# Projections and attention scores as fp16 half products, heads stacked by DMA, denominators from a ones column, no dummy matmuls

## What is computed

```python
x = x + conv(group_norm(x))          # two-way state scans over rows and columns, gated
t = tokens(x)                        # 16 x 1024 x 192
t = t + attn(layer_norm(t))
t = t + ffn(layer_norm(t))  # 4 experts 192 -> 768 -> 192, the best 2 per token, weighted
# attn: six heads of 32; token 0 sees all tokens, every other one sees token 0 and a window of 33
Q, K, V = x @ Wq + bq, x @ Wk + bk, x @ Wv + bv
s_rest  = einsum('bhld,bhlwd->bhlw', Q[:, :, 1:], Kw) / sqrt(32), masked
out     = concat(softmax(s_cls) @ V, softmax(s_rest) @ Vw) @ Wo + bo
```

## Time and profile before

| | us |
|---|---|
| median of three runs (lowest, highest) | 3214.75 (3212.38, 3215.9) |
| the profiled execution | 3210.95 |
| its span, first to last instruction | 3209.2 |
| TensorE busy in the span | 2742.2 (85%) |
| VectorE busy | 1883.9 (59%) |
| ScalarE busy | 1060.5 (33%) |
| GpSimd busy | 906.1 (28%) |

### The profile page before, as it was taken

The page is one execution under the profiler, slowest core; times in us unless marked ns, Lnnn a source line. Parts: engine busy times, 40 slices in busy tenths (PEclk is TensorE's granted clock), DMA queues, the critical chain, the costliest instruction groups (busy, mean ns, idle before and its releaser), DMA issues. The chain is left out here.

```text
span 3209.2 us, 50697 instructions
## 1 busy us (share of the span) xinstructions
PE 2742.2 (85%) x18097; PEld 2020.8 (63%) x18097; DVE 1883.9 (59%) x5344; ACT 1060.5 (33%) x3333; POOL 906.1 (28%) x672
## 2 busy tenths in 40 slices
PE   0478888998898999988998999998898989999597
PEld 0356575766667676666666676766667666766364
DVE  4454555666666566666656566566656566565464
ACT  0032423234242424334242424334242424334122
POOL 0001203050422415050422415050422415050544
PEclk9787978899998989999999989899998999899799
DMA  3430103132242415132242415133232415133564
GB/s 40 95 103 15 56 15 97 35 83 57 74 92 59 104 56 111 36 79 61 73 89 63 104 55 110 32 83 63 72 89 61 107 52 109 36 83 70 136 158 99
DMA packets 272634, 241.80 MB, mean 75 GB/s; under 512 B 209020, under 2 KB 250494, under 8 KB 261760
## 3 DMA queue, kind: packets, MB, share of 16 engines
q1 hardware_dynamic: 211648, 147.17, 17.9%
q0 software_dynamic: 50880, 52.59, 9.7%
q10 hardware_dynamic: 9856, 38.80, 3.8%
HBM read 133.29 MB, written 73.59 MB: 64 GB/s over the span
## 5 line engine op out<-in xcount | busy, mean ns | idle before, releaser
L1504 PE MATMUL PSUM<-XT,WB 128*128 128x512 f16 x2010 | 528.2, 396 | 24.5 <-DMA META<-slots 24.5
L795 ACT ACTIVATE HF<-PSUM,WB 128x512 f32<-128x512 f32 x402 | 275.8, 686 | 799.5 <-PE PSUM L1504 796.5
L1522 PE MATMUL PSUM<-WB,HHI 128*128 128x192 f16 x1608 | 404.2, 251 | 75.6 <-DVE HLO L1043 74.3
L818 ACT ACTIVATE PSPT<-PSUM,NMX 94x126 f32<-94x126 f32 x1056 | 366.9, 358 | 307.7 <-PE PSUM L1563 250.2
L1040 DVE TENSOR_SCALAR HHI<-HF 128x512 f16<-128x512 f32 x402 | 180.7, 450 | 407.3 <-ACT HF L795 404.2
L693 POOL DMA_INDIRECT out_dram<-Y,META x228 | 359.4, 1576 | 200.9 <-DVE Y L1068 117.6
L1524 PE MATMUL PSUM<-WB,HLO 128*128 128x192 f16 x1608 | 404.3, 251 | 0.0
L1523 PE MATMUL PSUM<-WB,HHI 128*128 128x192 f16 x1608 | 404.3, 251 | 0.0
L1504 PEld LDWEIGHTS PSUM<-XT,WB 128*128 128x128 f16 x2010 | 199.3, 103 | 197.6 <-issue 37.6
L1551 PE MATMUL PSUM<-KBD,QT 128*94 128x378 f32 x704 | 291.0, 495 | 18.8 <-ACT PSPT L818 17.2
L1043 DVE SCALAR_TENSOR_TENSOR HLO<-HF,HHI 128x512 f16<-128x512 f32 x402 | 282.6, 703 | 13.8
(11 more groups left out here) (269 smaller groups left out, 4978.5 us busy)
## 6 DMA issues: line engine op xcount, KB each, us to landing
WB<-weights SPq DMA_DIRECT2D x67, 1600.0 KB, 7.0
XR<-in_x ACTq DMA_DIRECT2D x16, 768.0 KB, 5.8
out_dram<-X ACTq DMA_DIRECT2D x32, 384.0 KB, 2.4
weights<-WB ACTq DMA_DIRECT2D x4, 1600.0 KB, 6.4
GUP<-TGU SPq DMA_DIRECT2D x256, 8.0 KB, 1.8
slots<-XROW,IDX POOLq DMA_INDIRECT x256, 2.4
out_dram<-Y,META POOLq DMA_INDIRECT x228, 3.6
HF<-in_w ACTq DMA_DIRECT2D x6, 384.0 KB, 4.6
```

The lines of the kernel that those rows point to most:

```text
L795: act.activation(HF[:, k % 2, :], PSUM[:, 4 + k % 2, :], ACT.Gelu, scale=1 / (X_UP * W_UP), bias=bias).then_inc(f["gelu_done"], 1)
L818: e = act.activation(PS[0:QS, n % 2, h, :], PSUM[0:QS, n % 2, h * KS:(h + 1) * KS], ACT.Exp, bias=NMX[:, b, n % 2, h:h + 1], accum_out=DEN ...
L1504: mm = pe.matmul(dst, WB[:, ws, w:w + 128], XT[:, xs, chunk, :], start=(n == 0), stop=(n == 4))
L1522: pe.matmul(dst, HHI[:, k % 2, tok], w2h, start=False, stop=False, skip_group_check=True)
```

## The change

- **Halves.** VectorE writes XN as fp16 rows of an upper half and the rest (XNR). TensorE turns these (24 fp16 transposes in place of 16 in f32), and XW holds three chunks of 128 rows. The weights are split in the same way once, at the start (WQKV).
- **Projections.** Each product is five fp16 matmuls (`X_CHUNK`) in place of two in f32.
- **Evacuation.** ScalarE evacuates all twelve Q and K pieces, each twice: as f32 (QKF) and as the upper fp16 half. VectorE subtracts them to get the lower half (`split_qk`) and evacuates all six V pieces, 33 columns for each head, of which the last stays at one.
- **Moves.** KBD is gone. `qk_moves` on SyncE copies the halves of each head into QST (upper, upper, lower) and KST (upper, lower, upper), stacked to 96 rows: 36 DMAs an image, in four groups of nine after the splits 3, 6, 9 and 12. The attention waits for all of them.
- **Scores.** The mask comes first, then one fp16 matmul for each head, 126 columns.
- **Denominators.** The exponentials no longer accumulate. The ones column of VW gives the sums with the values; VectorE copies token 0's row of them and takes the reciprocal from PSUM, behind the values.
- **Dummies.** The `keep_busy` of the attention is gone. That of image 0's conv stays.
- `STEPS` and the `empty` steps are shifted a little, and some buffers share space (XNR and the halves of K lie in X2 and XN).

```diff
-        STEPS = [(1, 1) if n < 16 else (2, 1) if n < 20 else (2, 2) for n in range(NSEL * HK)] + [(1, 1)]
+        STEPS = [(1, 1) if n < 16 else (2, 1) if n < 18 else (2, 2) for n in range(NSEL * HK)] + [(1, 1)]
...
+        X_CHUNK = (0, 0, 1, 2, 1)
...
+        def evacuate_qk(act, n):
+
+            oh, parts = piece_parts(n)
+            bias, scale = (BQS, HD ** -0.5 * UNSCALE) if n < 6 else (BK, UNSCALE)
+            for ps, plain, hi, lo in parts:
+                act.activation(plain, ps, ACT.Identity, bias=bias[:, oh:oh + 1], scale=scale)
+                last = act.activation(hi, ps, ACT.Identity, bias=bias[:, oh:oh + 1], scale=scale)
+            last.then_inc(s["piece_act"], 1)
+
+        def split_qk(dve, n):
+
+            for ps, plain, hi, lo in piece_parts(n)[1]:
+                last = dve.tensor_tensor(lo, plain, hi, ALU.subtract)
+            last.then_inc(s["qk_split"], 1)
...
+            def qk_moves(i):
+                for to, halves, rows in ((QST, [QHL[:, :, 0], QHL[:, :, 1]], (0, 0, 1)), (KST, KHL, (0, 1, 0))):
+                    for oh in range(2):
+                        sp.wait_ge(s["qk_split"], at("qk_split", i, 3 * oh + (3 if to is QST else 9)))
+                        for h in range(HH):
+                            for g, v in enumerate(rows):
+                                sp.dma_start(to[g * HD:(g + 1) * HD, oh * HH + h, :, :],
+                                             halves[oh][h * HD:(h + 1) * HD, v, :, :]).then_inc(s["qk_moved"], 16)
...
                 state_moves(i + 1)
                 expert(i, 3)
+                qk_moves(i + 1)
...
+                for k in range(2):
+                    tiles = slice(4 * k, 4 * k + 4)
+                    dve.wait_ge(s["xn1_ready"], at("xn1_ready", i, k + 1))
+                    link(dve.tensor_scalar(XNR[:, tiles, 0:C], XN[:, tiles, 0:C], X_UP, None, ALU.mult))
+                    dve.scalar_tensor_tensor(XNR[:, tiles, C:2 * C], XN[:, tiles, 0:C], X_UP, XNR[:, tiles, 0:C],
+                                             ALU.mult, ALU.subtract).then_inc(s["xnr_ready"], 1)
...
                 def normalize(b):
-                    dve.wait_ge(s["exp_done"], at("exp_done", i, 2 * b + 2))
-                    link(dve.reciprocal(RDEN[:, b, :, :], DEN[:, b, :, :]))
                     dve.wait_ge(s["pv_done"], at("pv_done", i, b + 1))
...
+                    dve.tensor_copy(DEN[:, b, :, :].rearrange("p a h -> p (a h)"), o[0:1, :, HD])
+                    link(dve.reciprocal(RDEN[:, b, :, :].rearrange("p a h -> p (a h)"), o[:, :, HD]))
...
-                    for j in range(2):
-                        mm = pe.matmul(PSUM[0:HC, n % 4, 0:width], W[:, j, oh * HC:(oh + 1) * HC],
-                                       XW[:, j, b0:b1, keys], start=(j == 0), stop=(j == 1))
+                    for m, c in enumerate(X_CHUNK):
+                        mm = pe.matmul(PSUM[0:HC, n % 4, 0:width], WQKV[:, kind, m, oh * HC:(oh + 1) * HC],
+                                       XW[:, c, b0:b1, keys], start=(m == 0), stop=(m == 4))
...
+                pe.wait_ge(s["qk_moved"], at("qk_moved", i, PER["qk_moved"]))
...
-                    pe.matmul(PSUM[0:QS, n % 2, 0:HH * KS], QT[:, oh, b, :],
-                              KBD[:, oh, b, :, :].rearrange("p h k -> p (h k)"), start=True, stop=False)
...
-                    pe.matmul(PSUM[0:QS, n % 2, 0:HH * KS], EYEB[:], MASKB[:, v, :], start=False, stop=True
-                              ).then_inc(s["score_done"], 1)
+                    pe.matmul(PSUM[0:QS, n % 2, 0:HH * KS], EYEB[:], MASKB[:, v, :], start=True, stop=False,
+                              skip_group_check=True)
+                    for h in range(HH):
+                        mm = pe.matmul(PSUM[0:QS, n % 2, h * KS:(h + 1) * KS], QST[:, oh * HH + h, b, :],
+                                       KST[:, oh * HH + h, b, :], start=False, stop=True, skip_group_check=True)
+                    mm.then_inc(s["score_done"], 1)
...
-                        keep_busy(8 if b == 1 else 2)
```

More of the change, by code:

```diff
@@ L30 @@
 QS = QB + 1
+VC = HD + 1
 E, HID = 4, 768
@@ L461, in hybrid_kernel, with windows @@
         STEPS_AHEAD = 1
-        STEPS = [(1, 1) if n < 16 else (2, 1) if n < 20 else (2, 2) for n in range(NSEL * HK)] + [(1, 1)]
-        def windows(copy, j, part, give):
+        STEPS = [(1, 1) if n < 16 else (2, 1) if n < 18 else (2, 2) for n in range(NSEL * HK)] + [(1, 1)]
+        def windows(copy, c, part):
             if part == 0:
[L469 to L475, removed]
+                return copy(XW[:, c, 1:NB - 1, 0:KW],
+                            window_view(PSUMH, c * T + QB - PAD + 1, [128, [QB, NB - 2], [1, KW]]))
+            copy(XW[:, c, 0, PAD - 1:KW], window_view(PSUMH, c * T, [128, [1, KW - PAD + 1]]))
+            copy(XW[:, c, NB - 1, 0:T - LAST_KEY], window_view(PSUMH, c * T + LAST_KEY, [128, [1, T - LAST_KEY]]))
+            return copy(XW[:, c, :, KW], window_view(PSUMH, c * T, [128, [0, NB]]))
@@ new lines, in piece_parts @@
+        def piece_parts(n):
+            src, oh, (b0, b1) = bank(n % 4), n // 3 % 2, SPANS[n % 3]
+            k, w = b1 - b0, QB if n < 6 else KS
+            hi, lo = ((QHL[:, v, oh, b0:b1, 1:QS] if n < 6 else KHL[oh][:, v, b0:b1, :]) for v in range(2))
+            plain = QKF[:, n % 2, 0:k * w].rearrange("p (b q) -> p b q", b=k)
+            parts = [(src[0:HC, 0:k * w].rearrange("p (b q) -> p b q", b=k), plain, hi, lo)]
+            if n < 6 and n % 3 == 2:
+                parts.append((src[0:HC, 400:401].broadcast_to((HC, NB)), QKF[:, n % 2, k * w:k * w + NB],
+                              QHL[:, 0, oh, :, 0], QHL[:, 1, oh, :, 0]))
+            return oh, parts
@@ L1202, in gates @@
                 dve.wait_ge(s["route_exp"], at("route_exp", i, 0))
+                if not (isinstance(i, int) and i == B):
+                    dve.wait_ge(s["mixed"], at("mixed", i, 1))
                 link(dve.tensor_reduce(sm1, se, AX.X, ALU.add))
@@ L1448, in conv @@
                         yield
-                yield from empty(4)
+                yield from empty(6)
                 pe.wait_ge(s["mixed"], at("mixed", i, NT))
@@ L1462, in conv @@
                     yield
-                yield from empty(3)
+                yield from empty(4)
                 pe.wait_ge(s["win_act"], at("win_act", i, 1))
@@ L1767, with thirds @@
     mask[0, 0, :, KW] = 0.0
+    def thirds(w):
+        w = w.reshape(3, C // 3, -1)
+        return np.stack([np.concatenate([w[p], w[q]], 0) for p, q in ((0, 1), (2, 0), (1, 2))], 1)
     w1, w2 = a["L1_ffn_w1"], a["L1_ffn_w2"]
@@ L1785 @@
         scan_v=sv, scan_u=su, scan_a=sa,
-        wq=halves(a["L1_attn_Wq"]), wk=halves(a["L1_attn_Wk"]), wv=halves(a["L1_attn_Wv"]), wo=np.concatenate([halves(a["L1_attn_Wo"]), wo_rows]),
+        wqkv=np.stack([thirds(a["L1_attn_W" + n]) for n in "qkv"], 1), wo=np.concatenate([halves(a["L1_attn_Wo"]), wo_rows]),
         bq=vec(a["L1_attn_bq"]), bk=vec(a["L1_attn_bk"]), bv=vec(a["L1_attn_bv"]),
```

196 lines of the change are left out of this document (105 added, 91 removed).

## The result

The changed kernel takes 3424.78 us (median of four runs, 3417.75 to 3426.27) against 3213.57 us (3209.22 to 3215.9): 1.0655 times, 95% interval 1.0635 to 1.0674. It is slower by 211 us. The profiled execution took 3426.27 us, its span is 3423.4 us, and TensorE's mean granted clock fell from 0.920 to 0.767.

A forecast was written before the change was run, and what follows sets the result against it. TensorE was taken to bound projections and attention. Fourteen images at -9.8 + 6.8 + 9.5 + 2.5 = +9.0 us (+126), plus +29 for images 0 and 1, gave 3370 us; forecast's own range 3310 to 3430, overall 3110 to 3440.

The forecast's parts named there:

- Projections: Projections stretch: eight matmul units become five, so it shortens from 33.4 to 23.5 us, -9.8 us an image.
- The moves: Ahead of the attention: 36 SyncE moves at 0.64 us each make TensorE wait 6.8 us an image.
- The clock: Attention: TensorE at half clock from the start, turns of 4.5 us, 56.2 us in all, +9.5 us.
- The rest: Stretches behind the attention and ahead of the projections: cold start and longer low clock, 1.7 to 3.5 us, value 2.5.
- the splits: Two VectorE splits into halves ahead of the transposes, some 1.5 us each: costed at 0, up to +3 in the range.
- The swinging between the levels: Attention: the clock swings between its levels instead of staying low, giving only part of the +9.5 us.
- The branch not taken: Attention at full clock: VectorE bounds turns of 3.3 to 3.5 us, 45.2 us in all, -1.5 us.
- The sum: Steady image: -9.8 + 6.8 + 9.5 + 2.5 = +9.0 us; images 0 and 1 +14.3 each; 3370 us in all.
- A: Rival: neither wait for moves nor fall of the clock, -10.8 us an image, 3045 us; chance 0.12.
- D: Rival: moves hidden at 0.43 us each, clock still falls, +2.7 us an image, 3260 us; chance 0.16.
- B: Rival: moves late but the attention's clock holds, -4.5 us an image, 3153 us; chance 0.10.
- E: Rival: moves at 0.96 us, or clock down through the 24.9 us behind the attention, 3510 to 3540 us; chance 0.08.

The follow-up runs named there:

- run 1: Changed kernel with the moves and the wait for them kept for image 0 alone, no dummies in the ring: 3290.22 us.
- Run 6: Changed kernel with the same 36 moves, each carrying 6 of the 11 windows (55% of the bytes): 3423.84 us.
- run 8: Changed kernel with dummies back (eight in the first turn, two in others) and eight of 36 moves done as VectorE copies: 3255.67 us.
- run 9: As run 8, with ScalarE's load of the next pixels held until the moves have landed: 3294.23 us.
- run 2: Changed kernel with the dummies back in the ring (eight in the first turn, two in the others), moves and wait unchanged: 3307.43 us.
- run 3: Changed kernel with moves for image 0 alone and the dummies back in the ring: 3170.59 us.
- run 5: Kernel before with the fp16 projections alone (halves, fp16 transposes, five matmuls), no moves, f32 scores and dummies kept: 3146.26 us, 0.9814 times the kernel before.
- run 10: As run 5, with the transposes of the halves one step later in the order: 3115.57 us, one run.
- run 12: The kernel of run 10 again, timed in five rounds: 3126.87 us, 0.9732 times the kernel before.
- run 4: Kernel before without the 28 dummies of each attention, f32 scores kept: 3239.22 us.

## Why the prediction was right, point by point

- **Projections: right.** Predicted 23.5 us for the 18 pieces with the FFN beside them, -9.8 (its terms, 15.1 and 8.2, add up to 23.3); measured 23.6 in every steady image. ScalarE's double evacuation fits, as computed: it is busy 16.69 us and the pieces wait for nothing.
- **The moves: right, a little small.** First move 5.9 us after the start of the projections, 0.64 each, landing 1.4 later, a wait of 6.8; measured 5.5, 0.675, 1.9 and 8.1. For the landing would have given 1.7 (2.3 less the 0.60 in the queue). Of the 8.1 us, 1.5 are no price of the moves, since run 1 has them too; the prediction has no such term. Run 6 shows that the price is per DMA, and the nearest row gave it well, in a range of waits from 0.5 to 18. The Trainium skill (DMA: Bandwidth & Descriptors, Issuing engines are not separate DMA queues) calls the time to initiate a DMA usually small beside the DMA. Here it is the bound: 0.675 us for each of 36 moves in a row, where the last lands 1.9 us after its issue. Its other sentence, that DMAs of all issuing engines interleave on the same 16 DMA engines, agrees with runs 8 and 9: beside ScalarE's load the last move lands after 4.8 us, without it after 2.4.
- **The clock: right.** Forecast 0.50 from the start of the attention with turns of 4.5 us and 56.2 us in all; measured 0.50, 4.43 and 55.1. The reason given had two parts, and run 1 parts them: the ring alone loses the clock, the wait only adds its own time. The swinging between the levels that the prediction weighed against it didn't come in the changed kernel; it shows with the dummies back, in runs 2 and 3 (in run 3 the clock falls to 0.50 twice and comes back, 0.81 over the attention). The branch not taken was also sized nearly right: a turn at full clock is 3.26 us (run 3), 3.3 to 3.5 predicted.
- **The rest: a cold start of the right size, and the splits, wrongly put at 0.** The rest grew by 4.6 us in the median; 2.5 were predicted, all for a cold start behind the attention. The cold start is in the trace: from the end of the attention the clock stays at 0.50 for 4.1 us, and the first matmul of the router comes after 27.3 us, where image 3 of the kernel before has 25.5 at 1.00. In the medians it is 27.7 against 25.6, so 2.1 us.

```profile
1411.30:1415.40 4.10, 3.28 (x16) 2.48 (x17) 1.75 (x7) 2.14 (x5) 0.00 (x0) 0.50 0.00 0
1411.30:1438.58 27.28, 23.17 (x159) 16.01 (x159) 19.61 (x51) 9.11 (x15) 1.01 (x1) 0.92 0.06 19
```

```profile
766.65:792.11 25.46, 21.58 (x159) 14.89 (x159) 19.26 (x49) 9.06 (x15) 1.01 (x1) 1.00 0.07 20
```

  The rests of runs 1, 3 and 5 (104.5, 105.0, 105.6) can't price a cold start, though their attentions have clocks of 0.52, 0.81 and 1.00: in run 5, too, the clock falls behind the attention.

```profile
1276.60:1280.50 3.90, 3.29 (x17) 2.44 (x17) 1.50 (x5) 2.11 (x5) 0.00 (x0) 0.56 0.00 0
```

  The splits ahead of the transposes are the step that was mis-sized. This is the place in the changed kernel (timeline of TensorE):

```profile
1509.17 1.44 PE L1515 MATMUL PSUM<-EYEH,X 128*128 128x128 f16 x12 [3.02 <-DVE X L1069]
1511.88 1.46 PE L1515 MATMUL PSUM<-EYEH,X 128*128 128x128 f16 x12 [1.27 <-DVE X L1069]
```

  TensorE waits 4.3 us there for the chain of ScalarE's normalizing and VectorE's splits, where the kernel before waits 2.5 to 3.2 us for the normalizing alone, and the clock over these ten us is 0.56 (0.84 over 11 us before). The first wait is 0.5 us longer, and from the first transpose to the projections it is 9.8 us in the median in place of 8.3: the splits and their transposes cost 2.0, of which 1.6 are waiting. The 0.5 us that are left lie between the router and the transposes. There the clock stays at 0.50 for 10 us in some images and for 20 in others, which moves the rest of an image by 3 to 4 us, so a smaller difference of two medians says little. In run 5 a shift of the order by one step takes 1.4 us back in image 6, 2.6 to 2.8 in the medians (runs 10 and 12).
- **The sum: right in its range, 55 us short in its value.** Predicted +9.0 us in a steady image; measured +12.6 (193.6 - 181.0). Of the 3.6 us by which it missed, 1.9 lie between the projections and the attention (-1.1 in place of -3.0, most of it the longer wait), 2.1 in the rest, and the attention gave 0.5 back (+9.0 in place of +9.5). For images 0 and 1 +14.3 was predicted; measured +19.1 and +17.1. Their clock was priced right (12.4 and 11.7, for 12), but the stretch to the attention grew by 6.7 and 5.4 us in place of 2.3, because the first move comes 6.7 us after the start, not 4.9, and in image 0 the moves then take 25.9 us, not 23. Image 2 belongs to these two and not to the steady ones: in the kernel before its projections run without FFN too (26.5 us), and it grew by 14.8. These three with 51 us, images 3 to 14 with 157, image 15 with 5 and the start with 2 give 215, and the profiled difference is 3426.27 - 3210.95 = 215. The time is 5 us below the top of the forecast's own range, so a little luck is in it. Of the rivals, A and D fell with the wait, B with the clock, and E with the pace of 0.675 and a clock that is back 4 to 7 us behind the attention.

## What to carry to other kernels

Count the DMAs that a step issues on one queue, not only their bytes: 36 moves at 0.675 us were a wait of 8 us that half of the bytes hardly shortened. Where matmuls get cheaper and an engine behind them becomes the bound, read what keeps TensorE's clock up, and price the step at the lower clock too: a turn of the ring cost 3.26 us at one level (run 3, with two dummies in it) and 4.43 at the other. And time the parts of a change apart: here the projections alone are 1.9% faster, 2.7% with their transposes a step later, while the whole is 6.6% slower. Not timed apart were the ones column for the denominators, and moves issued from a second engine.

## What the runs showed of the hardware that was not expected

- With 28 dummies in an attention that starts at half clock, TensorE comes back to full clock (run 2: 0.50 over the first 6 us, 0.87 over the rest). I had taken it to stay down.
- Leaving the dummies out of the f32 ring made it no shorter (46.5 against 46.1 us), although TensorE was the bound there; the fall of the clock to 0.98 takes back part of what they cost, and the stretch behind starts at 0.50 (run 4). Where the rest went was not settled.
- A move of 87 KB within SBUF took 0.59 to 0.61 us in SyncE's queue in the median, as did one of 8 KB. The last one landed 1.9 us after SyncE was done, or 4.8 when a 768 KB load had been issued on another engine's queue 7.7 us before SyncE was done.
